# Routing logits from fp16 high and low parts, with a range check of the router weights, and the tokens transposed one expert sooner

## The reference

```python
logits = xf @ Wg + bg                       # 128 features -> 8 experts
probs = jax.nn.softmax(logits, axis=-1)
w, idx = jax.lax.top_k(probs, TOP_K)        # TOP_K = 2
w = w / jnp.sum(w, axis=-1, keepdims=True)
comb = jnp.sum(jax.nn.one_hot(idx, E, dtype=xf.dtype) * w[..., None], axis=1)
h = jax.nn.relu(jnp.einsum('nd,edh->enh', xf, W1) + b1[:, None, :])
y = jnp.einsum('enh,ehd->end', h, W2) + b2[:, None, :]
out = jnp.einsum('end,ne->nd', y, comb)
```

## Time and the profile before

| what | us |
|---|---|
| median of 3 runs | 817.69 (816.82 to 818.20) |
| the profiled execution | 817.37 |
| its span, first to last instruction | 815.6 |
| PE busy | 768.8, 94% of the span |
| DVE busy | 648.0, 79% |
| ACT busy | 722.4, 89% |
| POOL busy | 560.4, 69% |
| granted TensorE clock, mean over the span | 0.993 |

### The profile page before, as it was taken

One profiled execution on the slowest core, in us unless ns is written; L12 is line 12 of the kernel. 1 busy time (PEld: TensorE's weight loads), 2 busy tenths in 40 slices (PEclk: granted clock), 3 DMA queues, 4 the chain that ended last, 5 costly groups with the idle time before them and its releaser, 6 DMA issues.

```text
span 815.6 us, 20389 instructions
## 1 busy us (share of the span) xinstructions
PE 768.8 (94%) x7673; PEld 423.1 (52%) x7673; DVE 648.0 (79%) x1901; ACT 722.4 (89%) x930; POOL 560.4 (69%) x685
## 2 busy tenths in 40 slices
PE   5799999999999999999999999999999999999996
PEld 4346666667776233333333333333334677777774
DVE  7898999888787667787777877788555999888885
ACT  5918989889989999999999999999997898999984
POOL 2888675554435988889888888888885455444442
PEclk9899999999999999999999999999999999999998
DMA  9110000000043233434433334423400000000000
GB/s 276 48 72 33 1 2 2 1 2 2 2 102 93 71 92 100 78 93 104 105 98 89 95 88 95 98 68 102 105 1 2 1 14 15 14 15 15 14 15 17
DMA packets 37962, 45.70 MB, mean 56 GB/s; under 512 B 6137, under 2 KB 23810, under 8 KB 37858
## 3 DMA queue, kind: packets, MB, share of 16 engines
q1 hardware_dynamic: 37858, 44.33, 21.1%
HBM read 27.53 MB, written 16.78 MB: 54 GB/s over the span
## 4 chain that ended last, share of the span: by engine, by line
PE 65%; ACT 16%; issue 9%; DVE 8%; POOL 1%; DMA 0%; ACTq 0%; DVEq 0%; POOLq 0%
PE psum L971 19%; PE psum L902 17%; ACT prob L1239 13%; PE psum L1283 12%; PE psum L1230 5%; PE psum L1341 4%; DVE mixed L990 2%; PE psum L1121 1%; PE psum L776 1%; PE psum L674 1%; DVE prod L644 1%; DVE hidden_parts_first L925 1%; ACT hidden_first L916 1%; PE psum L634 1%; PE psum L751 1%
## 5 line engine op out<-in xcount | busy, mean ns | idle before, releaser
L1239 ACT ACTIVATE prob<-psum 128x1536 f32<-128x1536 f32 x256 | 347.5, 1503 | 14.3 <-PE psum L1230 14.3
L1246 POOL TENSOR_SCALAR_AFFINE_SELECT prob<-prob 128x512 f32<-128x512 f32 (+3 forms) x448 | 304.7, 708 | 43.2 <-ACT prob L1239 33.1
L1283 PE MATMUL psum<-prob,vstack 128*32 128x256 f32 (+1 forms) x2048 | 204.9, 495 | 1.6 <-DVE o_tok L1291 1.6
L902 PE MATMUL psum<-xt_parts,w_parts 128*128 128x512 f16 x768 | 186.6, 379 | 0.0
L990 DVE SCALAR_TENSOR_TENSOR mixed<-psum,comb_y,mixed 128x128 f32<-128x128 f32 x512 | 143.3, 340 | 1.5 <-PE psum L971 1.5
L932 POOL TENSOR_TENSOR hidden_parts_second<-hidden_second,hidden_parts_second 128x512 f16<-128x512 f32 x64 | 77.3, 1208 | 94.4 <-ACT hidden_parts_second L918 94.3
L932 POOL TENSOR_TENSOR hidden_parts_first<-hidden_first,hidden_parts_first 128x512 f16<-128x512 f32 x64 | 77.9, 1220 | 66.6 <-ACT hidden_parts_first L918 66.4
L1230 PE MATMUL psum<-qstack,kstack 32*128 32x512 f16 x768 | 99.8, 385 | 8.2 <-ACT prob L1239 6.8
L916 ACT ACTIVATE hidden_second<-psum,b 128x512 f32<-128x512 f32 x128 | 88.3, 689 | 20.4 <-PE psum L902 16.6
L1230 PEld LDWEIGHTS psum<-qstack,kstack 32*128 32x128 f16 x768 | 24.9, 91 | 156.4 <-ACT prob L1239 137.7
L902 PEld LDWEIGHTS psum<-xt_parts,w_parts 128*128 128x128 f16 x768 | 72.0, 99 | 64.1 <-issue 1.4
(11 more groups left out here) (135 smaller groups left out, 848.3 us busy)
## 6 DMA issues: line engine op xcount, KB each, us to landing
qstack<-qk_parts SPq DMA_DIRECT2D x128, 128.0 KB, 3.5
qk_parts<-parts SPq DMA_DIRECT2D x64, 192.0 KB, 3.1
kstack<-qk_parts SPq DMA_DIRECT2D x128, 32.0 KB, 3.5
stream<-u_folded SPq DMA_DIRECT2D x4, 512.0 KB, 8.1
kept_x<-stream SPq DMA_DIRECT2D x4, 512.0 KB, 2.7
out<-mixed SPq DMA_DIRECT2D x7, 256.0 KB, 2.4
w_whole<-L_ffn_W SPq DMA_DIRECT2D x1, 1024.0 KB, 9.1
taps<-c_taps SPq DMA_DIRECT2D x1, 640.0 KB, 7.2
```

What stands on the lines that cost most here:

```text
L902: last = e.matmul(bank(u % 4), m.w1[:, w_part, ex, cols], xt_parts[:, s, x_part, :], start=(n == 0), stop=(n == len(PRODUCTS) - 1))
L1239: e.activation(prob[:, n % PROBS, :], psum[:, TILE * (n % 2):TILE * (n % 2 + 1)], ACT.Exp, scale=SCALE)\
L1246: return e.affine_select(kept, kept, [[0, kept.shape[1]], [0, 2], [sign, P]], ALU.is_ge, 0.0, base=0, channel_multiplier=-sign)
L1283: last = e.matmul(to[SLOT * lane:SLOT * (lane + 1)], vstack[:, b % 2, keys, first:first + SLOT], weights_of(n - t, lane, keys, pair), star ...
```

## The change

The router weights are scaled by 1024 and cut into an fp16 high part (ACT) and low part (DVE) in `wg_parts`, during the convolution. The logits of every chunk except the very first come from the parts. For each tile, one matmul multiplies the tokens' high part by both parts of the weights side by side (16 columns), and a second adds the tokens' low part times the weights' high part (8 columns). PE then waits for `xt_high`, `xt_low` and `wg_cut` ahead of the logits. DVE's one addition of `bg` becomes two dependent instructions that scale, add the bias and add the second half.

```diff
+WG_SCALE = 1024.0
+        e.mul(wg_parts[:, 0:EXPERTS], wg[:], WG_SCALE).then_inc(wg_high, 1)
+    def vector_cut_routing(e):
+        e.wait_ge(wg_high, 1)
+        e.scalar_tensor_tensor(out=wg_parts[:, EXPERTS:], in0=wg[:], scalar=WG_SCALE, in1=wg_parts[:, 0:EXPERTS],
+                               op0=ALU.mult, op1=ALU.subtract).then_inc(wg_cut, 1)
...
+    def logits_whole(m, ch):
+        return m.whole or (m is first and ch == 0)
     def tensor_logits(e, m, ch):
         n, s = m.at + ch, ch % 2
         e.wait_ge(xt_copied, n + 1)
-        if m is second and ch == 0:
+        if not m.whole:
             e.wait_ge(xt_high, n + 1)
+        if not logits_whole(m, ch):
+            e.wait_ge(xt_low, n + 1)
+            e.wait_ge(wg_cut, 1)
         if n:
             e.wait_ge(based, n)
         for i in range(FFN_TILES):
-            last = e.matmul(bias_bank(m, ch)[:, i * EXPERTS:(i + 1) * EXPERTS], xt[:, s, i * P:(i + 1) * P], wg[:], start=True,
-                            stop=True)
...
+                to = bias_bank(m, ch)[:, 2 * i * EXPERTS:2 * (i + 1) * EXPERTS]
+                e.matmul(to, xt_parts[:, s, 0, tile], wg_parts[:], start=True, stop=False)
+                last = e.matmul(to[:, 0:EXPERTS], xt_parts[:, s, 1, tile], wg_parts[:, 0:EXPERTS], start=False, stop=True)
...
+            e.scalar_tensor_tensor(out=logits[:, s], in0=made[:, :, 0], scalar=1.0 / WG_SCALE, in1=bias, op0=ALU.mult,
+                                   op1=ALU.add).then_inc(logits_begun, 1)
+            e.wait_ge(logits_begun, n)
+            e.scalar_tensor_tensor(out=logits[:, s], in0=made[:, :, 1], scalar=1.0 / WG_SCALE, in1=logits[:, s],
+                                   op0=ALU.mult, op1=ALU.add).then_inc(routed, 1)
```

```diff
     def routing_step(ch, ex):
 
-        return ex - 1 if ch == 1 else ex
+        return (None, None, 0, None, 2, 3, 5, 6)[ex] if ch == 1 else ex
```

More of the change, by code:

```diff
@@ L775, in tensor_logits @@
         for i in range(FFN_TILES):
-            last = e.matmul(bias_bank(m, ch)[:, i * EXPERTS:(i + 1) * EXPERTS], xt[:, s, i * P:(i + 1) * P], wg[:], start=True,
-                            stop=True)
+            tile = slice(i * P, (i + 1) * P)
+            if logits_whole(m, ch):
+                last = e.matmul(bias_bank(m, ch)[:, i * EXPERTS:(i + 1) * EXPERTS], xt[:, s, tile], wg[:], start=True,
+                                stop=True)
+            else:
+                to = bias_bank(m, ch)[:, 2 * i * EXPERTS:2 * (i + 1) * EXPERTS]
+                e.matmul(to, xt_parts[:, s, 0, tile], wg_parts[:], start=True, stop=False)
+                last = e.matmul(to[:, 0:EXPERTS], xt_parts[:, s, 1, tile], wg_parts[:, 0:EXPERTS], start=False, stop=True)
         last.then_inc(logit_up, 1)
@@ L781, in vector_top @@
         n, s = m.at + ch, ch % 2
+        bias = bg[:].rearrange("p (a e) -> p a e", a=1).to_broadcast([P, FFN_TILES, EXPERTS])
         e.wait_ge(logit_up, n + 1)
-        e.tensor_tensor(logits[:, s], bias_bank(m, ch)[:, 0:FFN_TILES * EXPERTS].rearrange("p (t e) -> p t e", e=EXPERTS),
-                        bg[:].rearrange("p (a e) -> p a e", a=1).to_broadcast([P, FFN_TILES, EXPERTS]), ALU.add)\
-         .then_inc(routed, 1)
+        if logits_whole(m, ch):
+            e.tensor_tensor(logits[:, s], bias_bank(m, ch)[:, 0:FFN_TILES * EXPERTS].rearrange("p (t e) -> p t e", e=EXPERTS),
+                            bias, ALU.add).then_inc(routed, 1)
+        else:
+            made = bias_bank(m, ch)[:, 0:2 * FFN_TILES * EXPERTS].rearrange("p (t k e) -> p t k e", k=2, e=EXPERTS)
+            e.scalar_tensor_tensor(out=logits[:, s], in0=made[:, :, 0], scalar=1.0 / WG_SCALE, in1=bias, op0=ALU.mult,
[3 more added lines that the diff above has]
+                                   op0=ALU.mult, op1=ALU.add).then_inc(routed, 1)
         e.wait_ge(routed, STEPS * n + 1)
@@ L1038, in vector_range @@
             e.reduce_max(extent[:, 0:2], widest[:].rearrange("p (n e) -> p n e", n=2), AX_X)
-            for at, part in ((2, wqkv_parts[:, 0].rearrange("p g d -> p (g d)")), (3, b1[:])):
+            for at, part in ((2, wqkv_parts[:, 0].rearrange("p g d -> p (g d)")), (3, b1[:]), (4, wg_parts[:, 0:EXPERTS])):
                 last = e.tensor_reduce(extent[:, at:at + 1], part, AX_X, ALU.max, apply_absolute_value=True)
@@ L1043, in vector_range @@
             e.wait_ge(range_up, 1)
-            e.reduce_max(extents[:], bank(7)[0:1, 0:4 * P].rearrange("a (n p) -> a n p", p=P), AX_X).then_inc(ranged, 1)
+            e.reduce_max(extents[:, 0:4], bank(7)[0:1, 0:4 * P].rearrange("a (n p) -> a n p", p=P), AX_X).then_inc(ranged, 1)
         elif step == EXPERTS + 2:
             e.wait_ge(ranged, EXPERTS + 2)
-            e.tensor_scalar(within[:, 0:3], extents[:, 0:3], W_MIN * WSCALE, None, ALU.is_ge).then_inc(ranged, 1)
+            e.wait_ge(counted, 3)
+            e.tensor_scalar(within[:], extents[:], W_MIN * WSCALE, None, ALU.is_ge).then_inc(ranged, 1)
             e.wait_ge(ranged, EXPERTS + 3)
+            e.scalar_tensor_tensor(out=within[:, 4:5], in0=extents[:, 4:5], scalar=W_MAX * WSCALE, in1=within[:, 4:5],
+                                   op0=ALU.is_le, op1=ALU.mult)
             e.scalar_tensor_tensor(out=within[:, 0:3], in0=extents[:, 0:3], scalar=W_MAX * WSCALE, in1=within[:, 0:3],
@@ L1397, in vector_conv @@
         vector_residual(e, 2)
+        vector_cut_routing(e)
         e.wait_ge(s_expw, EXPW)
```

32 lines of the change are left out of this document (18 added, 14 removed).

## The result

The changed kernel takes 822.79 us (median of 4 runs, 822.19 to 823.84) against 817.69 before. The ratio is 1.0067, with a 95% interval of 1.0055 to 1.008: 5 us slower. Its profiled execution took 823.84, the longest of the four, with a span of 822.1.

A forecast was written before the change was run, and what follows sets the result against it. PE bounds steady second experts, a DVE, POOL, PE chain the first, DVE both chunks 0. Terms -3.6 - 1.0 - 0.6 - 0.3 + 2.9 + 1.2 + 0.2 = -1.2 gave 816.2 to 816.5, stated 816.3; range 813.0 to 819.4.

The forecast's parts named there:

- The logits' call: Eight pairs on PE: 0.25 us in place of 0.85, 30 ns a pair, saving 0.60 a call (0 to 0.75).
- The rivals in which the pairs keep a pace of 56 ns or more: Logits on PE: 56 ns a pair gives 818.1 (chance 0.10); no cheaper logits, over 819.3 above 70 ns (0.12).
- Term 6: First experts, chunk 0: comb_t waits for DVE's comb_parts, at about 85.8; +2.9 us (+1.9 to +3.6).
- Term 7: Second experts, chunk 0: more DVE work stands before comb_parts, ready at 645.2; +1.2 us (0.4 to 1.6).
- Term 8: Weight cuts, two short instructions before the first chunk, and the check's additions at the end: +0.2 us (0 to 0.4).
- Term 1: Second experts, chunks 1 to 6: one cheaper logits call each, DVE staying ahead; 6 x 0.60, -3.6 us.
- The rival of a spent slack: Second experts: comb_parts late, PE waits 0.4 to 0.5 in each of six chunks; 819.0 us, chance 0.08.
- term 3: First experts, chunks 1 to 5: POOL's lows hit DVE elsewhere; -0.2 a chunk, -1.0 us (0 to 0.6 each).
- Terms 3 and 4: First experts: chunks 1 to 5, -1.0 us; chunk 6, where attention's preparation keeps PE nearly full, -0.6 (0 to 0.6).
- the second rival: First experts: chunk 0 costs +1.9, the DVE chain shifts with PE in chunks 1 to 5 (-3.0); 813.7 us, chance 0.27.
- Term 5: Attention's last batch, one logits call, PE and ACT near even: half of 0.60, -0.3 us (0 to 0.6).

The follow-up runs named there:

- experiment 5: The changed kernel with DVE's cut of the router weights moved behind the first chunk's combine: 822.07 us, ratio 1.0057.
- experiment 4: The changed kernel with 20 and 15 matmuls, results overwritten, filling PE's wait ahead of comb_t of chunk 1 (first, second experts): 819.66 us, ratio 1.0017.
- kernel 2: The kernel before, still with fp32 logits, with only the routing steps moved as in the change: 829.60 us, ratio 1.0151.
- experiment 9: kernel 6 with xt back at expert 1 in chunks 2 to 7: 815.56 us, ratio 0.998.
- experiment 7: kernel 6 with 7 matmuls, results overwritten, in PE's wait of 2.0 us behind the last up of chunk 1, first experts: 814.20 us, ratio 0.9958.
- kernel 10: kernel 6 with three accumulating matmuls for each tile and one DVE instruction fewer, and xt back at expert 1 in chunks 2 to 7: 816.17 us, ratio 0.9981.
- kernel 6: The changed kernel with fp32 logits at their old place in chunks 0 and 1, attention's last batch as before, weight cut late: 814.26 us, ratio 0.9959.
- kernel 1: The changed kernel's fp16 logits, weight cut and range check, with every routing step at its place in the kernel before: 821.23 us, ratio 1.0036.
- kernel 3: The changed kernel, but chunk 1 of both stages keeps fp32 logits and the combine at its old expert: 815.47 us, ratio 0.9969.

## Why the prediction was wrong

It forecast 816.3 and a range of 813.0 to 819.4; the time is 822.79.

- **The logits' call** was right and a little cautious: 0.20, not 0.25, 25 ns for each pair. The rivals in which the pairs keep a pace of 56 ns or more are out. On this point the trace sides with the floor of about 25 ns in the Trainium skill (TensorE: Matmul & The Clock Gate, section Wait — 56ns, not 53.3ns?), and not with the 81 ns a pair of the same page's section Back-to-back issue gap.
- **Term 6, chunk 0 of the first experts: the mechanism was right, the sum lacked the clock.** `comb_parts` was forecast at 85.8; it came at 87.36, and 1.6 of that is the late start: 85.8. (So close a match is partly luck: in experiment 5, with a start only 0.17 late, comb_t starts at 86.37, where the forecast would put it at about 86.0.) From there the step "then comb_t (0.11), up 1.29, down 1.34" failed. They took 0.13, 2.56 and 2.38. +5.3 in place of +2.9, of which 2.3 is the clock, measured by experiment 4.
- **Term 7, chunk 0 of the second experts**: the same. The wait was foretold as about 4 us (3.74). The down at 648.20 of before starts at 656.78, 8.58 later, of which 5.73 was there at comb_t of chunk 0: +2.85 in place of +1.2, and 1.6 of that is the clock (5.88 less 4.24, experiment 4). Without it the term was right.
- **"The granted clock is 1.00 ... and I expect no change of it"** is thus the sentence that failed. The prediction itself foretold waits of 4.5 and 4 us, longer than any in these stages of the trace of before, where 1.64 was the longest and the clock stayed. It priced the waits and took the work behind them at full speed. The clock is the largest term, but not all: without its 4.1 us, by the sum below, the profiled execution would be 819.7, and the median of experiment 4 is 819.66, both just above the range.
- **Term 8, +0.2**, was 1.1 for the cut alone. The instruction costs 0.2; what it moved was the start of the copy behind it, into POOL's access (experiment 5).
- **Term 1, -3.6**: it is 8.58 to 6.80, -1.8. Five of the six chunks gave 0.66 each, a little more than the 0.60 of the forecast. The one between the bases of chunks 2 and 3 lost 1.5 (9.45 less 7.92). There PE waited 0.82 for POOL's low and 0.80 at comb_t, which the prediction had named as a sign of being wrong. The rival of a spent slack had its number wrong, one chunk and not six, and did not name the cause: it is the sooner xt, as experiments 2 and 9 show. "Moving xt an expert sooner costs PE nothing" (term 3) does not hold in chunk 2 of either stage.
- **Terms 3 and 4, -1.6**, came out as 6.89 to 5.60, -1.3, but by other parts: 0.56 on average for each of the four later chunks, more than the 0.2 forecast for three of them, 0.5 for the chunk before, and +1.46 between the bases of chunks 2 and 3. Of this 1.46, the clock behind the wait of 1.99 makes 0.2 (experiment 7) and the sooner xt the rest (experiment 9). The wait ahead of a down, foretold to grow from 1.38 to 1.8, is 1.37 to 1.48 in the later chunks: the chain over DVE and POOL moved along with PE, as the second rival had it. What in that chain moved is argued, not shown by a run.
- **Term 5, -0.3**: +0.1 in the trace, and a loss of about 3 in one of experiment 4.

Added up for the profiled executions, where the span grew by 6.5 and -1.2 was forecast, a miss of 7.7: the clock 4.1 (2.3, 1.6 and 0.2), term 1 1.8, chunk 2 of the first experts without the clock 1.5, the copy 0.9, the start 0.5, attention 0.4, the rest of term 6 0.1; against that 1.3 more from the other first chunks and 0.3 at the end (6.80 to 6.5). That is 7.7.

What stays open: whether the gaps of 0.93 and 0.95 in the last attention batch cost the clock in a given execution, and so how much of the change's spread they make. It was seen in one profile, and no run was made for it alone. They can't be the only such place: the kernel before, which has one of the two gaps, took from 816.3 to 821.5 in 29 executions, and those above 821 have a mean granted clock of 0.989 where most others have 0.992 or more; kernels 9 and 10, with the old order in that batch, reach 819.5 and 818.8. Nor is it shown why one wait costs the clock and another of the same length does not: 1.99 in the changed kernel and in kernel 6, 2.12 in kernel 9 and 2.13 in kernel 1, 3.74 in the changed kernel and in kernel 5.

## What to carry to other kernels

When a forecast contains a wait of several microseconds on TensorE, price what comes behind it at the lower clock as well, here up to as much again as the next two or three microseconds of work, as a part of the range: it came behind five of the six waits of 3.7 us and more. Then ask whether something else would have held TensorE soon after; where it would, 1.7 us of slow work cost 0.2. If work on TensorE gets cheaper only with inputs that come later, keep the dear form where they are late (here the first two chunks) and use the cheap one where they are early: that gave 814.3, and 813.5 with one more matmul in place of a dependent DVE instruction, where the change for all chunks gave 822.8. And of a new short instruction, ask what it delays into another engine's access, not how long it is.

## What the hardware showed that I had not expected

- Eight pairs of an fp16 weight load of 128 columns and a matmul of 16 or 8 columns take 0.20 us, 25 ns a pair, where the fp32 form took 106 ns for each of 8 records.
- The waits of PE of 4.89, 4.96 and 4.90 us were each followed by matmuls at the lower clock, 2.3 us more for an up and a down in the changed kernel. So were 3.74 in the changed kernel (1.6 us more) and 3.71 in kernel 2, but not 3.74 in kernel 5; 2.58 and 2.12 in kernels 1 and 9, but not 2.64 and 2.13 in kernel 1; 1.99 in the changed kernel and kernel 3, but not in kernel 6. One of 1.64 was not in the kernel before.
- A DVE copy of 0.28 lasts 1.25 when it starts together with an instruction of POOL of 1.16, and 0.28 when it starts 0.14 ahead of it.
